# Cross-attention block with residual and LayerNorm: a different start, a different order in the second half of each step, and different last operations

## What is computed

```python
Q = heads(query @ w_q.T + b_q)      # query: 4 x 1024 x 256, 16 heads of 16
K = heads(ctx   @ w_k.T + b_k)      # ctx:   4 x 64 x 256
V = heads(ctx   @ w_v.T + b_v)
scores = Q @ K.T / 4                # 64 keys
scores = where(mask == 0, -1e9, scores)
attn = softmax(scores)
out = merge(attn @ V) @ w_o.T + b_o + query
mu, var = mean(out), var(out)       # over the 256 features
out = (out - mu) * rsqrt(var + 1e-5) * gamma + beta
```

## Time and profile before

| what | us |
|---|---|
| median of three executions | 165.19 |
| the profiled execution, its own time | 164.33 |
| its span, first to last instruction | 162.5 |
| mean granted TensorE clock | 0.964 |

### The profile page before, as it was taken

How to read it: one execution, slowest core, us unless ns; L and a number is a source line. 1 busy time by engine, 2 the same in 40 slices (tenths; PEclk the granted TensorE clock), 3 DMA queues, 4 the chain that set the end, 5 groups by cost and what they waited for, 6 DMA issues and landing times.

```text
span 162.5 us, 2904 instructions
## 1 busy us (share of the span) xinstructions
PE 137.3 (84%) x992; PEld 87.0 (54%) x992; DVE 124.9 (77%) x231; ACT 94.7 (58%) x166; POOL 115.5 (71%) x111
## 2 busy tenths in 40 slices
PE   0798975989899998999899989998999579999400
PEld 0676853746556655565556565655665335468300
DVE  0263899348788897989798979898989797999951
ACT  3349687593963666766676675846763815640220
POOL 5003741029999539999999999999981899667783
PEclk9999999699999999999999999999999999999955
DMA  4988983999927886006730940048003503003024
GB/s 119 342 234 198 283 197 85 317 244 269 287 71 187 314 217 252 0 0 196 180 148 0 224 167 0 2 105 274 12 2 76 187 0 129 0 4 122 7 94 166
DMA packets 10175, 23.21 MB, mean 143 GB/s; under 512 B 1584, under 2 KB 1840, under 8 KB 10160
## 3 DMA queue, kind: packets, MB, share of 16 engines
q1 hardware_dynamic: 9584, 22.03, 46.7%
q10 hardware_dynamic: 576, 0.99, 1.9%
HBM read 14.62 MB, written 4.19 MB: 116 GB/s over the span
## 4 chain that ended last, share of the span: by engine, by line
PE 45%; DVE 15%; POOL 14%; issue 7%; DMA 7%; SPq 6%; ACT 3%; POOLq 1%; DVEq 0%
PE ps_w L436 11%; PE ps_w L357 9%; PE ps_w L331 8%; DMA m_sb<-maskT 7%; PE ps_s L385 6%; PE ps_s L412 5%; POOL y L873 5%; DVE nmax L667 4%; POOL y L876 4%; DVE turned L688 3%; SPq L215 3%; PE ps_s L391 3%; ACT y L585 2%; DVE cn L701 2%; POOL rstd L857 2%
## 5 line engine op out<-in xcount | busy, mean ns | idle before, releaser
L667 DVE TENSOR_REDUCE nmax<-ps_w 128x8 f32<-128x512 f32 x56 | 37.7, 678 | 15.2 <-PE ps_w L357 14.8
L572 ACT ACTIVATE probs<-ps_s 128x512 f32<-128x512 f32 x64 | 33.1, 602 | 18.3 <-PE ps_s L396 18.3
L810 POOL TENSOR_TENSOR xt_l<-xt_sb,xt_h 128x1024 fp32r<-128x1024 f32 x7 | 16.6, 2374 | 30.6 <-ACT xt_h L533 19.8
L436 PE MATMUL ps_w<-wo_sb,cn 128*128 128x256 f32 x112 | 29.3, 387 | 3.9 <-DVE cn L701 3.6
L357 PEld LDWEIGHTS ps_w<-k_half,q_mask 128*128 128x128 f32 x112 | 17.3, 190 | 25.5 <-DVE nmax L667 19.7
L357 PE MATMUL ps_w<-k_half,q_mask 128*128 128x256 f32 x112 | 27.9, 335 | 3.2 <-DVE nmax L667 2.9
L436 PEld LDWEIGHTS ps_w<-wo_sb,cn 128*128 128x128 f32 x112 | 19.3, 189 | 9.2 <-DVE cn L701 5.5
L585 ACT ACTIVATE y<-res,shift,rstd 128x256 f32<-128x256 f32 x28 | 14.8, 590 | 12.6 <-POOL shift L859 12.5
L873 POOL TENSOR_TENSOR y<-y,brow 128x512 f32<-128x512 f32 x14 | 17.9, 1279 | 4.5 <-ACT y L585 4.1
L688 DVE STREAM_TRANSPOSE turned<-ps_s 128x1024 f32<-128x1024 f32 x16 | 19.8, 1240 | 0.8 <-PE ps_s L412 0.8
L844 POOL TENSOR_TENSOR x_sb<-x_sb,brow 128x1024 f32<-128x1024 f32 x8 | 19.1, 2382 | 0.1
(11 more groups left out here) (75 smaller groups left out, 203.3 us busy)
## 6 DMA issues: line engine op xcount, KB each, us to landing
m_sb<-maskT SPq DMA_DIRECT2D x32, 128.0 KB, 3.5
q_mask<-mask SPq DMA_DIRECT2D x32, 128.0 KB, 2.6
x_sb<-x SPq DMA_DIRECT2D x8, 512.0 KB, 4.3
xt_sb<-xT SPq DMA_DIRECT2D x7, 512.0 KB, 4.4
out<-y SPq DMA_DIRECT2D x6, 512.0 KB, 3.4
xt_sb<-xT SPq DMA_DIRECT2D x2, 256.0 KB, 5.7
out<-xt_sb SPq DMA_DIRECT2D x2, 256.0 KB, 2.0
brow<-bias_rows SPq DMA_DIRECT2D x1, 384.0 KB, 6.4
```

The source lines that it names most:

```text
L436: return pe.matmul(tile_outputs(c, i)[:, t], cn[:, c % 2, j, (2 * i + t) * P:(2 * i + t + 1) * P], wo_sb[:, j], start=j == 0 and c < LAST, ...
L572: act.activation(probs[:, g % 2, quad], ps_s[:, quad], ACT.Exp).then_inc(e_done, 1)
L667: dve.tensor_reduce(nmax[:, c % 2, t].rearrange("p (q r) -> p q r", r=32)[:, :, 2 * j:2 * j + 2], max_bank(c, i).rearrange("p (q h k) -> p ...
```

## The change

**Start.** The mask of chunk 0 is also loaded into a new tile `m_first`, ahead of `load_xt(1)` and `wv`, and DVE writes its values straight into `q_mask` (`first_mask_values`, two operations of 64x1024), so `copy_mask(0)` is gone. `mask_values(0)` stands behind the keys. `project_values` is sixteen products of 64 keys by 128 columns, into two banks by half, where it was eight of 128 by 256, and all stand ahead of `max_scores(0, 0)`. ACT's `high_x(1)` stands ahead of `first_queries_out(0)`. `mask_values(2)` and `value_blocks` (now two operations) move from behind the maxima of chunk 0 to behind the third maximum of chunk 1.

**Second half of a step.** PE: `values(s, 0)` behind the first maximum product; the two output tiles come one maximum product later. DVE: `residual(s-1, 0)` behind the seventh maximum (the third of this half), `moments(s-1, 0)` behind the eighth.

**Ends.** In the last step the output tiles of chunk 5 come ahead of `values(6, 1)` on PE, and `residual(5, 1)`, `moments(5, 1)` ahead of `divide(6, 1)` on DVE. POOL does `last_deviations(0)` ahead of the second half of `deviations(6)`. Semaphore counts follow.

```diff
@@ sync
-            load_mask(0)
-            sp.dma_start(wv_sb[:], wv).then_inc(in_wv, 16)
-            load_xt(1)
-            copy_mask(0)
+            for half in range(2):
+                sp.dma_start(m_first[rows(half)], maskT[0]).then_inc(in_mfirst, 16)
+            load_xt(1)
+            sp.dma_start(wv_sb[:], wv).then_inc(in_wv, 16)
+            load_mask(0)
             load_mask(1)
@@ tensor
+            def project_values():
+
+                pe.wait_ge(in_wv, 16)
+                for b in range(BATCHES):
+                    for d in range(PC):
+                        for h in range(2):
+                            mm = pe.matmul(projected_values(h)[:, b], ctx_t[:, d, b],
+                                           wv_sb[:, d].rearrange("p (q e) -> p q e", e=32)[:, :, 16 * h:16 * h + 16],
+                                           start=d == 0, stop=d == PC - 1)
...
                 if i == 0:
-                    pe.wait_ge(mk_in[c % 2], 16 * QUADS * (c // 2 + 1))
+                    if c == 0:
+                        pe.wait_ge(mfirst_done, 2)
+                    else:
+                        pe.wait_ge(mk_in[c % 2], 16 * QUADS * (c // 2 + c % 2))
...
-            project_values(0)
-            project_values(1)
-            project_values(2)
+            project_values()
             max_scores(0, 0)
-            project_values(3)
             max_scores(0, 1)
...
                 if s == LAST:
-                    values(LAST - 1, 1)
                     output(LAST - 2, 1, 0)
                     output(LAST - 2, 1, 1)
+                    values(LAST - 1, 1)
                     scores(LAST, 1)
...
                 max_scores(front, 4)
                 if s >= 1:
-                    output(s - 1, 0, 0)
+                    values(s, 0)
                 max_scores(front, 5)
                 if s >= 1:
+                    output(s - 1, 0, 0)
+                max_scores(front, 6)
+                if s >= 1:
                     output(s - 1, 0, 1)
-                max_scores(front, 6)
-                values(s, 0)
+                else:
+                    values(s, 0)
                 max_scores(front, 7)
@@ scalar
+            high_x(1)
             first_queries_out(0)
-            high_x(1)
             first_queries_out(1)
@@ vector
+            def first_mask_values():
+                dve.wait_ge(in_mfirst, 32)
+                for half in range(2):
+                    r = rows(1 - half)
+                    dve.tensor_scalar(q_mask[r, 0, half], m_first[r].unsqueeze(1).to_broadcast([64, 2, CHUNK]), 0.0, -BIG,
+                                      ALU.is_equal, ALU.mult).then_inc(mfirst_done, 1)
...
             first_low_x()
-            mask_values(0)
+            first_mask_values()
...
             first_half_keys()
+            mask_values(0)
             for i in range(HALVES):
                 maxima(0, i)
                 if i == 3:
                     mask_values(1)
-            mask_values(2)
-            value_blocks()
...
                 maxima(front, 2)
                 if s >= 2:
                     moments(s - 2, 1)
+                elif s == 0:
+                    mask_values(2)
+                    value_blocks()
...
                 maxima(front, 5)
+                maxima(front, 6)
                 if s >= 1:
                     residual(s - 1, 0)
-                maxima(front, 6)
+                maxima(front, 7)
                 if s >= 1:
                     moments(s - 1, 0)
-                maxima(front, 7)
                 divide(s, 0)
-            divide(LAST - 1, 1)
             residual(LAST - 2, 1)
             moments(LAST - 2, 1)
+            divide(LAST - 1, 1)
@@ gpsimd
             affine(LAST - 1, 0)
+            last_deviations(0)
             deviations(LAST - 1, slice(2, 4))
-            last_deviations(0)
             last_deviations(1)
```

More of the change, by code:

```diff
@@ L81, in build @@
         mask = sb("mask", [P, NM, 2, CHUNK], F32R)
+        m_first = sb("m_first", [P, CHUNK], I32)
         q_sb = sb("q_sb", [P, NQ, 2, CHUNK])
@@ L159, in max_bank, with projected_values @@
             return ps_s[:, 2 + i % 2] if c == 0 else ps_w[:, 0] if beside(c, i) else ps_w[:, 1]
-        def value_bank(b):
-            return (ps_c, ps_d)[b // 2]
+        def projected_values(h):
+            return (ps_c, ps_d)[h][rows(h), 0].rearrange("k (b p e) -> k b p e", b=BATCHES, e=16)
         def values_banks(g):
@@ L190, in deviations_done @@
         def deviations_done(c, second):
-            return 4 * (c + 1) if c < LAST - 2 else 4 * (LAST - 2) + 4 * (2 * (c - LAST + 2) + second + 1)
+            if c < LAST - 2:
+                return 4 * (c + 1)
+            halves = 2 * (c - LAST + 2) + second + 1
+            return 4 * (LAST - 2) + (4 * halves if halves < 4 else 18 if c < LAST else 14 + 6 * second)
         def new_batch(step):
@@ L671, in value_blocks @@
             def value_blocks():
-                dve.wait_ge(v_done, BATCHES)
+                dve.wait_ge(v_done, 2 * BATCHES)
                 dve.wait_ge(fill_done, 5)
                 dve.wait_ge(in_bv, 16)
-                for h, b, n, first in ((0, 0, 2, 0), (0, 2, 2, 2), (1, 0, 2, 1), (1, 2, 1, 3), (1, 3, 1, 0)):
+                for h in range(2):
                     r, e = rows(h), slice(16 * h, 16 * h + 16)
                     dve.tensor_tensor(
-                        v_bd[r, first:first + n, :, e],
-                        value_bank(b)[r, 0].rearrange("k (b p e) -> k b p e", b=2, e=32)[:, b % 2:b % 2 + n, :, e],
+                        v_bd[r, :, :, e], projected_values(h),
                         brow[r, 0].rearrange("k (p e) -> k p e", e=32)[:, :, e].unsqueeze(1)
-                        .to_broadcast([64, n, PAIRS, 16]), ALU.add).then_inc(vbd_done, 1)
+                        .to_broadcast([64, BATCHES, PAIRS, 16]), ALU.add).then_inc(vbd_done, 1)
             def divide(c, j):
@@ L958 @@
         "ctxT": np.ascontiguousarray(
[L959 removed]
+            ctx.transpose(2, 0, 1).reshape(PC, P, BATCHES, KEYS).transpose(1, 0, 2, 3)),
         "wq": weight(L0_xattn_w_q), "wk": weight(L0_xattn_w_k),
```

23 lines of the change are left out of this document (8 added, 15 removed).

## The result

The changed kernel takes 171.49 us (median of four executions, 170.65 to 172.5); the kernel before, run on the same chip, takes 165.34 us (164.49 to 167.47). The ratio is 1.039, 95% interval 1.029 to 1.049: slower by more than 2%, and 1.6 us above the forecast of 169.9, inside the range. The profiled execution took 170.72 us, against 164.33 before: +6.39.

The account below looks back on a forecast made before the run. PE and POOL were taken to meet at 40.5 us, so a later POOL costs in full and a faster PE gains nothing; 2.3 + 1.3 + 1.75 + 0.2 = 5.55 on 164.33 gave 169.9 us, range 165.7 to 172.5.

Parts of the forecast that it names:

- Term 1: Start to batch 1: the later mask_values(2) delays the loads POOL waits for, +2.3 us (1.3 to 3.0).
- rival D: Start: POOL's low_x(1) takes the shared port before DVE's mask_values(0), +0.55 us more, 170.4 us; chance 0.2.
- Term 2: Behind PE's stand before batch 1: the clock falls to one half for 3.4 us, +1.3 us (0 to 2.5).
- term 3: Second half of steps 1 to 5: later residual and division, 0.35 us per step, +1.75 us (1.0 to 2.5).
- Rival C: Behind PE's stand at batch 1: the clock holds, so +4.25 us in all, 168.6 us; chance 0.14.
- Rival B: Second halves: each step gets shorter by PE's 0.47 us, +1.45 us in all, 165.8 us; chance 0.18.
- Term 4: The end: last_deviations(0) put first delays ACT's last two normalised operations by 1.06 us, total +0.2 us (0 to 0.4).
- Rival A: Start of batch 1: POOL's wait doesn't bind, so PE's 3.6 us come through, 162.7 us; chance 0.06.

Follow-up runs that it names:

- experiment 6: The changed kernel with twelve added matmuls of 128x512 between scores(1, 0) and the first maximum product of batch 1: 169.82 us, ratio 1.0284.
- experiment 3: The kernel before with only the new order in the second half of a step: 165.8 us, ratio 1.0049.
- experiment 1: The changed kernel with mask_values(2) and value_blocks back behind the maxima of chunk 0: median 167.78 us (164.27 to 169.92), no ratio.
- experiment 2: The changed kernel with the old order of PE and DVE in the second halves: 170.33 us, ratio 1.030.
- experiment 4: The changed kernel with only the load of brow[:, 1:4] issued ahead of copy_mask(2) on SP: 169.0 us, one execution.
- experiment 11: The kernel before with the changes of the ends alone: 165.38 us, one execution.
- experiment 7: The changed kernel with brow[:, 1:4], load_xt(3) and load_x(0) issued ahead of copy_mask(2), and the old order in the second halves: 163.02 us, ratio 0.986.
- experiment 8: The kernel before with brow[:, 1:4], load_xt(3) and load_x(0) issued ahead of copy_mask(2): 165.4 us (162.05 to 168.15), no ratio.
- Experiment 5: The changed kernel with brow[:, 1:4], load_xt(3) and load_x(0) issued ahead of copy_mask(2): 163.64 us, ratio 0.986.
- experiment 10: The changed kernel, three loads ahead of copy_mask(2), new second-half order in step 6 alone, mask_values(0) behind chunk 0's fourth maximum: 162.03 us, ratio 0.980.

## Why the prediction was right, and where it was not

The direction, the class and the mechanism came out as forecast, and the sum was short by 0.8 us against the profiled execution's own time and by 1.6 us against the median. By its terms, in the profiled execution:

| term | forecast (bounds), us | measured, us | how |
|---|---|---|---|
| 1, start to batch 1 | +2.3 (1.3 to 3.0) | +2.7 | 43.25 - 40.53 |
| 2, clock | +1.3 (0 to 2.5) | +2.6 | 7.13 - 4.53; experiment 6 |
| 3, second halves | +1.75 (1.0 to 2.5) | +1.0 | table of steps: 6.31, less 2.72 + 2.60; experiment 3 gives 1.0 too |
| 4, the end | +0.2 (0 to 0.4) | +0.1 | 27.68 - 27.59 |
| sum | +5.55 | +6.4 | spans 168.9 - 162.5 |

**Term 1: right, by its own chain, in the execution that was profiled.** `mask_values(2)` was to end at 27.7 and ended at 28.00; `half_keys(1)` was to end at 42.65 and ended at 43.14. Experiment 1 shows that the one move carries the term. The remaining 0.5 us: 0.3 at the mask, 0.2 behind it, where 14.94 us became 15.14. That it fits so well is in part luck. In experiments 2 and 6, the same program up to this stand, PE reaches batch 1 at 45.01 and 45.24, 4.5 and 4.7 us later than before and above my upper bound of 3.0, because the clock falls at the start. The forecast has no term for that: it counted the half-clock stretch of before as lost work that the change saves, and did not ask whether the new start makes another. The slower pair of after's own executions may be of this kind. Wrong was a detail of the start. I had DVE first and POOL's `low_x(1)` behind it at 14.3; the trace has POOL first, at 13.38, because the mask of chunk 0 had not landed when the keys were done (0.68 us). That is the mechanism of rival D, but not its price: D had `mask_values(1)` end at 19.95, 0.55 later than the forecast, and it ended at 19.69. POOL's earlier start (13.38, where D had 13.6) accounts for 0.22 of the 0.26 us between the two. The keys were done at 13.05 and not at 13.5, and the value products started at 11.62 and not at 12.52; neither helped, since DVE's first maximum waited for the mask operation.

Wrong, too, was the picture of PE's stand. I had it idle in one piece for 5 to 6 us from 36.7. In fact the idle time between 35 and 43.25 us is 1.97 + 0.66 + 2.93 = 5.56 us in three pieces, the first two through ACT's wait for x of chunk 3. I had listed `load_xt(3)` among what is queued behind `copy_mask(2)`, and followed only `brow`. It changed nothing in the sum, since POOL ended later still; with `brow` mended (experiment 4) it would have been the next to bind.

**Term 2: right in kind, half the size in this execution.** The step that missed is "I expect the same at 42.7": that the clock would stay low for 3.4 us, as before. It stayed low for 6.6 us, and the cost went to 2.60, just above my upper bound of 2.5, which rested on "nearly twice as long". But the 3.4 us are what the other traces show for a low stretch near this point (experiments 1, 2 and 4), at a cost of 1.53, 1.11 and 1.57 us, on both sides of the 1.3 forecast; the execution of after is the one that differs. Terms 1 and 2 together come to 5.6 us in experiment 2, with its late start and short low stretch, and to 5.3 in after; the forecast had 3.6. That the total came so close is therefore partly luck: term 3, 0.75 us too large, covers part of the gap. Rival C, the clock holds, is refuted in after and in experiment 2, where PE stands for 2.93 and 3.24 us.

**Term 3: right in sign, 0.6 times the size.** The chain on DVE was right: I expected the division 0.4 to 0.5 us later within the half, and it starts 91.27 - 85.72 = 5.55 us behind the first maximum, against 84.96 - 79.84 = 5.12, so 0.43. What I took too small is the slack that absorbs it. The division starts 3.00 us ahead of the next step's first maximum in after (91.27 to 94.27); in before that took 3.18 us (84.96 to 88.14), because DVE waited there for PE. That wait takes up 0.18 of the 0.43, which leaves 0.25, and the period of this step grew by 0.22 (16.21 to 16.43). The term was also counted five times at the same size, where step 5 adds only 0.04 us: the kernel before takes 16.38 us for that step by itself. Rival B, that the halves get shorter, is refuted by experiment 3 and by all five halves (8.69 to 8.78, against 8.36 to 8.60), except in step 6, where I had excluded it from the sum because the end hangs on POOL. That was right with the ends of before: in experiment 3 the stretch from `scores(6, 0)` to the last `affine` is 38.96 us, and 38.99 in before.

**Term 4: the total right, the reason wrong.** I costed ACT's last normalising operation against its spare 0.99 us. Experiment 11, one execution, shows +0.5 us for the ends alone, more than my upper bound, with waits for DVE's moments that I had not looked at. Measured from `scores(6, 0)` to the last `affine`, the ends alone take 39.49 us (experiment 11) and 39.51 (experiment 7), against 38.99 in before; with the new order in step 6 as well it is 39.11 in after. So the new order gives back 0.4 of it. The +0.1 in after is a difference of two effects, and each alone was outside what I wrote.

**Rival A**, POOL's wait does not bind, is refuted by the 2.93 us in PE's row at 43.25, whose releaser is `k_half`. In before the same wait was hardly binding (0.28 us at most, experiment 8): both engines met there, and a shift of POOL costs in full (after) while a gain of PE brings nothing (experiment 1), as the prediction had it. Experiment 5 is the counterproof.

On DVE and POOL at the start: the mask operation ends at 16.29, 0.55 us behind the end of POOL's operation at 15.74, as in before. The Trainium skill (SBUF — State Buffer, on the shared port pair) calls this an exclusive lock under which the second engine is blocked for the whole instruction; the trace agrees, with 2.55 us for an operation of 0.68.

## What to carry to other kernels

Before an operation is moved later on one engine, list what is queued in order behind its waiting consumer, DMA issue queues above all, and follow every engine that waits for each of those loads: here three loads that need nothing stood behind a copy that waited for a mask, and moving them ahead turned +3.9% into -1.4%. Where two engines arrive at one point together, cost a delay in full and a gain at nothing, and add the clock that an idle PE may lose. A reordering that removes one wait inside a step is worth only what the next wait in the same chain lets through, so follow the chain on both engines to the same point one period later.

## What the runs showed of the hardware that I had not expected

**An idle PE loses its clock, but not each time, and for how long varies.** Idle stretches of nearly one length went both ways. In the second half of step 6 PE waits 1.83 us for `cn` in both before and experiment 2. In before the clock stays at 1.00 from 123 to 138 us, as it does behind the same 1.83 us in experiments 7 and 11; in experiment 2 it fell (timeline and windows):

```profile
134.28 2.07 PE L447 MATMUL ps_w<-wo_sb,cn 128*128 128x256 f32 x4 [1.83 <-DVE cn L708]
```

```profile
135.00:136.00 1.00, 1.00 (x5) 0.82 (x3) 0.00 (x0) 1.00 (x3) 0.67 (x1) 0.50 0.00 0
```

That half took 11.34 us, against 9.83: 1.5 us from one wait. Experiment 8 showed the same half at 11.33. At the start, after kept its clock through a stand of 2.69 us (1.00 in the windows from 16 to 20 us), while in experiment 7 it fell around one of 2.09 us. Window of experiment 7:

```profile
18.00:19.00 1.00, 1.00 (x5) 0.81 (x5) 0.21 (x1) 0.00 (x0) 0.03 (x1) 0.50 0.84 281
```

There `scores(0, 0)` starts at 24.54 instead of 23.12, and the six other profiles named above show the same. It also fits the scatter of the changed kernel, whose four executions come in two pairs, 170.65 and 170.72 us at a mean clock of 0.966 and 0.961, 172.25 and 172.5 at 0.941 and 0.929; only one was profiled, so this is an inference. Low stretches lasted some 3.4 us elsewhere (in experiment 1 from 42.05 to 45.45) and 6.6 us behind the restart in after. What decides between these cases the runs do not say.

**The value products in two half-width tiles** took 1.97 us for 32 instructions of 128 columns, 0.062 us each, where 12 of 256 columns took 2.75. That was inside the bounds. No run takes this edit alone. In experiment 10 the collision behind it is gone and `scores(0, 0)` starts 1.1 us earlier than in before, but how much of that is the value products and how much the missing copy is not shown.
